# A perceiver block on one core: chunk 1's gathers behind the last gelu, chunk 0 sent to the scores first, two chunks' contexts loaded in four parts

## What is computed

```python
x = x + L0_xattn(layernorm(x), ctx, ctx, ...)        # 16 heads
x = x + L0_attn(layernorm(x), ...)                   # a state space convolution
# L0_ffn: the first mixture, 16 experts, each token goes to its best four
logits = -dist2(x, keys) + x @ rw.T + rb
topv, topi = jax.lax.top_k(logits, 4);  w = softmax(topv)
hidden = gelu(einsum('bld,efd->blef', x, w1) + b1)
exp_out = einsum('blef,edf->bled', hidden, w2) + b2
fused = sum(w[..., None] * take(exp_out, topi), axis=2);   x = x + fused
# L1_xattn: one head, masked, no projections
h = layernorm(x)
attn = softmax(where(mask == 0, NEG, h @ ctx.T / 16))
x = x + layernorm(attn @ ctx) * gamma + beta
x = x + L1_attn(layernorm(x), ...)                   # selective scan
x = x + L1_ffn(layernorm(x), ...)                    # 8 experts, best two, and a shared one
```

## Time and profile before

| | us |
|---|---|
| median of 3 runs (lowest, highest) | 712.33 (711.55, 713.86) |
| the profiled execution, its own time | 712.5 |
| its span, first to last instruction | 710.7 |
| outside the span | 1.8 |
| TensorE busy | 676.7 (95%) |
| VectorE, ScalarE, GpSimd busy | 543.6, 414.0, 452.4 |
| mean granted TensorE clock | 0.994 of full |

### The profile page before, as it was taken

One profiled execution on the slowest core, in us unless ns is written; L12 is line 12 of the kernel. 1 busy time (PEld: TensorE's weight loads), 2 busy tenths in 40 slices (PEclk: granted clock), 3 DMA queues, 4 the chain that ended last, 5 costly groups with the idle time before them and its releaser, 6 DMA issues.

```text
span 710.7 us, 15537 instructions
## 1 busy us (share of the span) xinstructions
PE 676.7 (95%) x5712; PEld 554.0 (78%) x5712; DVE 543.6 (76%) x1212; ACT 414.0 (58%) x790; POOL 452.4 (64%) x487
## 2 busy tenths in 40 slices
PE   6899999999999988999999999998899899999998
PEld 3677778777777767999999999996457456666787
DVE  5887878787889776577777777754647999998676
ACT  3665656656665653566667667641336886665441
POOL 4848635546487644888998787736315699898130
PEclk9999999999999998999999999999999999999999
DMA  8301101011006565899999989975874610001000
GB/s 343 129 2 61 61 1 59 6 53 60 0 0 252 209 242 240 317 365 414 422 348 331 347 334 333 346 305 193 325 310 156 249 51 1 0 1 46 1 0 30
DMA packets 20365, 123.38 MB, mean 174 GB/s; under 512 B 2304, under 2 KB 6672, under 8 KB 13008
## 3 DMA queue, kind: packets, MB, share of 16 engines
q1 hardware_dynamic: 17376, 114.59, 42.0%
q0 software_dynamic: 2928, 8.00, 3.1%
HBM read 111.77 MB, written 10.81 MB: 172 GB/s over the span
## 4 chain that ended last, share of the span: by engine, by line
PE 81%; DVE 9%; ACT 5%; issue 3%; POOL 1%; DMA 1%; DVEq 0%; SPq 0%; ACTq 0%; PEldq 0%; POOLq 0%
PE banks L2279 70%; PE banks L2347 8%; DVE shown L2145 2%; PE banks L2911 2%; ACT probs L1155 1%; DVE negmax_raw L1674 1%; PE banks L2588 1%; ACT banks L1445 1%; DVE banks L2152 1%; DMA table<-in_table 1%; DVE xn L1566 1%; PE banks L2747 0%; ACT turned_back L1456 0%; POOL q_heads_hi L713 0%; POOL rstd L701 0%
## 5 line engine op out<-in xcount | busy, mean ns | idle before, releaser
L2279 PE MATMUL banks<-xT,raw 128*128 128x128 f32 x992 | 150.5, 275 | 0.6 <-DVE xT L1932 0.6
L2279 PEld LDWEIGHTS banks<-xT,raw 128*128 128x128 f32 x992 | 133.6, 191 | 3.1 <-issue 1.3
L971 POOL TENSOR_TENSOR w_lo<-raw,w_hi 128x1024 fp32r<-128x1024 f32 x52 | 122.8, 2389 | 0.9 <-ACT w_hi L1275 0.5
L1306 ACT ACTIVATE banks<-banks,later 128x128 f32<-128x128 f32 x208 | 70.5, 340 | 58.1 <-PE banks L2279 56.3
L1938 DVE CAST mid_hi<-banks 128x128 fp32r<-128x128 f32 x208 | 60.2, 289 | 36.5 <-ACT banks L1306 34.4
L1185 ACT ACTIVATE probsT<-banks 128x512 f32<-128x512 f32 x68 | 40.1, 598 | 74.8 <-PE banks L2347 74.5
L1055 POOL TENSOR_TENSOR inject<-BCbc,drive 128x1024 f32<-128x1024 f32 x31 | 72.8, 2362 | 11.3 <-DVE shown L2145 6.5
L1155 ACT ACTIVATE probs<-banks,negmax 128x1024 f32<-128x1024 f32 x64 | 71.2, 1113 | 11.7 <-DVE negmax L1676 9.9
L1674 DVE TENSOR_REDUCE negmax_raw<-banks 128x1 f32<-128x1024 f32 x64 | 77.5, 1211 | 0.4 <-PE banks L2279 0.3
L2279 PE MATMUL banks<-w_hi,mid_hi 128*128 128x256 f32 x208 | 75.5, 363 | 0.0
L2347 PE MATMUL banks<-table,probs 128*128 128x128 f32 x512 | 69.6, 279 | 0.4 <-DVE probsT L1647 0.4
(11 more groups left out here) (362 smaller groups left out, 1707.7 us busy)
## 6 DMA issues: line engine op xcount, KB each, us to landing
raw<-in_w SPq DMA_DIRECT2D x31, 2048.0 KB, 10.0
ctx_raw<-in_ctxT SPq DMA_DIRECT2D x8, 1024.0 KB, 4.7
ctxT<-in_ctxT SPq DMA_DIRECT2D x4, 2048.0 KB, 8.8
ctxN<-in_ctxN SPq DMA_DIRECT2D x4, 2048.0 KB, 13.9
x_slots<-zero SPq DMA_DIRECT2D x1, 3968.0 KB, 12.5
y_slots<-y_tile POOLq DMA_DIRECT2D x29, 128.0 KB, 7.0
wf<-in_w SPq DMA_DIRECT2D x9, 384.0 KB, 5.9
BCbc<-bc_rows SPq DMA_DIRECT2D x6, 512.0 KB, 6.9
```

The costliest lines, as they stand in the source:

```text
L971: nc.gpsimd.tensor_tensor(w2_lo[i % WB][:, cols], raw[i % WB][:, EW // 2:][:, cols], w2_hi[i % 2][:, cols].bitcast(F32), ALU.subtract).the ...
L1306: nc.scalar.activation(to, held, ACT.Gelu, bias=b1[:, bass.ds(at + u, 1)]).then_inc(gelu_done, 1)
L2279: return nc.tensor.matmul(o, lhsT, rhs, start=start, stop=stop)
```

## The change

It edits four things, and the arithmetic is the same.

1. GpSimd: chunk 1's four gathers wait for all 248 gelus. The power of chunk 0 (`rstd_of(4, 0)`) moves from behind chunk 2's second gather to ahead of its first; the power of chunk 1 now stands behind chunk 2's second gather, and chunk 2's third and fourth gathers behind that power.
2. VectorE: `combine(1)` moves behind the end of chunk 0's norm (`arrive(0)`).
3. SyncE: T(1) is no longer issued at the stores but after `gathered[0]`.
4. SyncE: T(1), T(2) and N(1) are issued as four DMAs of 512 KB each. A part of T has runs of 2 KB (half the keys of one of two rows), a part of N runs of 4 KB, where one DMA had 8 KB for a partition and batch. The waits on them count 64 for the four in the place of 16.

The diff, cut to its core (the waits on T and N count `16 * CTX_T_PARTS[p]` and `16 * CTX_N_PARTS[p]` accordingly):

```diff
+CTX_T_PARTS, CTX_N_PARTS = (1, 4, 4, 1), (1, 4, 1, 1)
...
             def context_T(p):
-                sp.dma_start(ctxT2[p][:], d["ctxT"][2 * p:2 * p + 2].rearrange("b p c n -> p b c n"))\
-                    .then_inc(ctxT2_loaded[p], 16)
+                if CTX_T_PARTS[p] == 1:
+                    sp.dma_start(ctxT2[p][:], d["ctxT"][2 * p:2 * p + 2].rearrange("b p c n -> p b c n")).then_inc(ctxT2_loaded[p], 16)
+                    return
+                for b in range(2):
+                    for keys in (slice(0, KEYS // 2), slice(KEYS // 2, KEYS)):
+                        sp.dma_start(ctxT2[p][:, b, :, keys], d["ctxT"][2 * p + b][:, :, keys]).then_inc(ctxT2_loaded[p], 16)
...
+                for b in range(2):
+                    for of in (slice(0, KC // 2), slice(KC // 2, KC)):
+                        sp.dma_start(ctxN2[p][:, b, of, :], d["ctxN"][2 * p + b][:, of, :]).then_inc(ctxN2_loaded[p], 16)
...
                 if i == COLD - 1:
-                    sp.wait_ge(y_stored[i % YB], 16 * (i // YB + 1))
+                    sp.wait_ge(gathered[0], 16 * TOP0)
                     context_T(1)
...
             gather_rows(0)
+            pool.wait_ge(gelu_done, TILES * UNITS)
             gather_rows(1)
+            rstd_of(4, 0)
             pool.wait_ge(last_taken, last_before + LAST)
             gather_rows(2, range(2))
-            rstd_of(4, 0)
-            gather_rows(2, range(2, 3))
             rstd_of(4, 1)
-            gather_rows(2, range(3, TOP0))
+            gather_rows(2, range(2, TOP0))
             gather_rows(3)
...
             combine(0)
-            combine(1)
             add_sums(0, 1)
             norm_begin(4, 0)
             add_sums(1, TC)
+            arrive(0)
+            combine(1)
             norm_begin(4, 1)
-            arrive(0)
             arrive(1)
```

More of the change, by code:

```diff
@@ L599, in context_T @@
             def context_T(p):
-                sp.dma_start(ctxT2[p][:], d["ctxT"][2 * p:2 * p + 2].rearrange("b p c n -> p b c n"))\
-                    .then_inc(ctxT2_loaded[p], 16)
-            def context_N(p):
-                sp.dma_start(ctxN2[p][:], d["ctxN"][2 * p:2 * p + 2].rearrange("b p k n -> p b k n"))\
-                    .then_inc(ctxN2_loaded[p], 16)
+                if CTX_T_PARTS[p] == 1:
[4 more added lines that the diff above has]
+                        sp.dma_start(ctxT2[p][:, b, :, keys], d["ctxT"][2 * p + b][:, :, keys]).then_inc(ctxT2_loaded[p], 16)
+            def context_N(p):
+                if CTX_N_PARTS[p] == 1:
+                    sp.dma_start(ctxN2[p][:], d["ctxN"][2 * p:2 * p + 2].rearrange("b p k n -> p b k n")).then_inc(ctxN2_loaded[p], 16)
+                    return
+                for b in range(2):
+                    for of in (slice(0, KC // 2), slice(KC // 2, KC)):
+                        sp.dma_start(ctxN2[p][:, b, of, :], d["ctxN"][2 * p + b][:, of, :]).then_inc(ctxN2_loaded[p], 16)
             sp.wait_ge(pads_ready, 1)
@@ L2156, in _ @@
                     elif m == 0 and g <= SPLIT_ROWS:
-                        dve.wait_ge(c_landed[g - 1], raw_loads(1 + g) + 32)
+                        dve.wait_ge(c_landed[g - 1], raw_loads(1 + g) + 16 * CTX_T_PARTS[g] + 16)
                     elif m == 0:
@@ L2730, in score2 @@
                 k = p % 2
-                pe.wait_ge(ctxT2_loaded[p], raw_loads(p + 1) + 16)
+                pe.wait_ge(ctxT2_loaded[p], raw_loads(p + 1) + 16 * CTX_T_PARTS[p])
                 pe.wait_ge(early_ready, TC + p + 1)
@@ L2750, in mix2 @@
             def mix2(p):
-                pe.wait_ge(ctxN2_loaded[p], 48 if p == TC - 1 else 32)
+                pe.wait_ge(ctxN2_loaded[p], (32 if p == TC - 1 else 16) + 16 * CTX_N_PARTS[p])
                 pe.wait_ge(left2_ready, p + 1)
```

## The result

| | before | after |
|---|---|---|
| median, measured side by side, 16 runs each (lowest, highest) | 713.45 (711.55, 716.26) | 715.97 (713.51, 717.35) |
| ratio, 95% interval | | 1.0032 [1.0018, 1.0045] |
| the profiled execution, its own time | 712.5 | 715.07 |
| its span | 710.7 | 713.3 |
| mean granted TensorE clock | 0.994 | 0.995 |

The change makes the kernel slower by 0.32%, 2.3 us of the median and 2.6 between the two profiled executions. The interval reaches to both sides of 0.3%: that the kernel got slower is clear, whether by more than 0.3% is not. The two traces can be laid over each other without a shift: the first of ScalarE's two copies of the last tiles starts at 483.60 before and at 483.72 after.

What follows compares the result with a forecast made beforehand. TensorE was taken as the bound, held up by late signals to the gelus and by context loads. Loads 2.5 + 0.6 = 3.1 later, less slack 1.9, gave 1.2: 712.5 + 1.2 = 713.7, median 713.5, range 711.0 to 716.5.

Steps and rivals of the forecast that it cites:

- rival A: TensorE's signals late beside T(1) and chunk 1's gathers, 1.4 to 2.8 us slower: 714.9 to 716.3, chance 0.30.
- late loads set scores 3: T(3) lands 3.1 later against a slack of 1.9, so TensorE starts scores 3 1.2 later.
- one of its own signs of failure: The forecast fails if T(2) takes clearly more than 9.5 from first issue to last landing.
- The other signs: T(2) leaves at 502.5 to 503.5; TensorE idles about 2 ahead of mix 1, a little ahead of scores 3.
- the likeliest class: Whole kernel: time the same within 0.3%, chance 0.57, against faster 0.05 and slower 0.38.
- Late signals removed: From gelus to chunk 0's turn: gelus come in time, last sums at 490.7 not 492.37, 1.6 us gained.
- a pair, gathers and a load: End of the mixture: TensorE's signals reach ScalarE late, by some 4 us, while eight gathers and T(1) run together.
- Chunk 1's rows "are in" before VectorE wants them: On VectorE: the rows are in at 493.9, 2.9 after the last gather starts; combine(1) starts at 495.1.
- For T(1) the parts cost nothing: T(1) on SyncE: it starts at about 486 and is needed beyond 500, so its parts cost zero.
- Parts of T(2) and N(1): Context loads: four parts cost 0.5 for T(2) and 0.1 for N(1), 0.6 together, ends 0 to 1.6.
- My bound from the next stage's weights: Cost of parts: 2 MB take 5.78 at 363 GB/s, not 4.96 at 423, so 0.8 more per T.
- The queue behind chunk 1's power: On GpSimd: chunk 2's third and fourth gathers wait for chunk 1's power, so T(2) leaves 2.5 later.

Runs made afterwards that it cites:

- only_gelu_wait: The kernel before with one edit, chunk 1's gathers wait for the last gelu: 718.23, ratio 1.009 to the kernel before.
- only_t1_wait: The kernel before with one edit, T(1) waits for chunk 0's gathers: 716.42, ratio 1.0049 to the kernel before.
- t1_and_gelu_wait: The kernel before with both waits, T(1) behind chunk 0's gathers and chunk 1's gathers behind the last gelu: 717.52, ratio 1.0078.
- parts_off: The kernel after with T(1), T(2) and N(1) as one DMA each again: 714.65, ratio 1.0021 to the kernel before.
- only_parts: The kernel before with the four parts alone, waits and orders as before: 713.68, ratio 1.0019 to the kernel before.
- five_gathers: The kernel after with chunk 1's first gather issued directly behind chunk 0's four: 716.47, ratio 1.0036 to the kernel before.
- early_wait: The kernel after with chunk 1's gathers waiting for the fourth last gelu, not the last: 715.35, ratio 1.0025 to the kernel before.
- greatest_ahead: The kernel after with whole loads, chunk 2's four gathers ahead of chunk 1's power, and greatest(2) ahead of leave(0) on VectorE: 712.43, ratio 1.0002.
- greatest_again: The kernel of greatest_ahead run once more, unchanged: 711.35 beside 712.89 for the kernel before, ratio 0.9981.
- g2_ahead: The kernel after with all four gathers of chunk 2 ahead of chunk 1's power on GpSimd: 712.78, ratio 1.0003 to the kernel before.

## Why the prediction came out as it did

The forecast was 713.5 with its own range to 714.4, and the time 715.97 lies above that, inside the wide range of 711.0 to 716.5. That it lies inside is partly luck: the upper end was drawn for rival A, whose late signals did not come. The mechanism was the forecast's own (late loads set scores 3), but its terms were too small, and one of its own signs of failure came true: T(2) took 10.8 from its first issue, clearly more than 9.5. The other signs: T(2) left at 503.78, just outside 502.5 to 503.5; TensorE waited 1.45 ahead of mix 1 and 0.46 ahead of scores 3, each released by a load, where I had said about 2 and a little, and 1.64 ahead of scores 2, which I had not foreseen. Whether the likeliest class, no change within 0.3%, holds at 0.32% the interval leaves open.

- **Late signals removed: right.** Last sums 490.76 (forecast 490.7), turn at 495.63 (495.6), chunk 0's end on VectorE 495.05 (495.1).
- **Why they were late: half wrong.** I named a pair, gathers and a load. The load isn't needed: only_gelu_wait has the pair, with four gathers, and no late gelu; only_t1_wait has no load at the first late gelu and most of the delay (3.2 of 3.9 at the last gelu). The length of the row of gathers counts. Rival A with its 0.30 was built on the pair; its late signals between 489 and 495 did not come, beside T(1) and four gathers. Its price was misread too: the last gelu came 2.0, not 1.4, above the pitch behind the one ahead of it (2.49 of idle time against 0.51), and the 1.36 of the earlier trace rows is idle time, of which 0.85 is lateness.
- **Chunk 1's rows "are in" before VectorE wants them: wrong.** I took 2.9 from the last gather's start, a row of gathers that ran alone. Beside T(1) it was 495.90 - 491.35 = 4.5. That shifted the whole row by 0.8, and T(2) left 3.3 later instead of 2.5.
- **"For T(1) the parts cost nothing": wrong, and this is the same 0.8.** TensorE doesn't need T(1) early, but the gathers share the DMA engines with it. Among the kernels that have chunk 0 first, `combine(1)` waits 0.85, 2.21, 0.47 and 0.38 in the four with T(1) in parts and not at all in the five with it in one piece. Those rows were taken 10.1 to 11.4 after T(1)'s first issue; in only_t1_wait and t1_and_gelu_wait, where `combine(1)` waits beside a whole T(1), 9.2 after it. I had even written that short runs let a gather pass sooner; the rows came later beside them.
- **Parts of T(2) and N(1): 0.6 forecast, 1.1 measured** (20.8 against 19.7), 0.9 by parts_off and 1.6 by only_parts, where the slack covered it. My bound from the next stage's weights took runs of 3 KB for runs of 2 KB.
- **The queue behind chunk 1's power: right in kind.** Undone alone it gave back 2.1 us by the ratios, 1.3 by the trace at scores 3.
- **The wait ahead of mix 0 wasn't in the sum.** It grew from 0.83 to 1.73 in the profile, and to 2.20 to 2.84 in three sister kernels, with half clock behind it. The cause is late signals for the two copies `probsT` beside six gathers in a row: together they are 0.9, 1.4, 2.0 and 1.9 late in the kernel after, parts_off, five_gathers and early_wait, which is what the wait exceeds 0.83 by. Where the loads don't cover it, as in parts_off, it is what remains.
- **The sum with measured terms:** 3.3 + 1.1 - 1.9 = 2.5 in place of 1.2; 712.5 + 2.5 = 715.0, and the profiled execution took 715.07. The median of the 16 runs is 0.9 above it, where I had set 0.2 below. Five of those 16 have a mean granted clock of 0.988 or 0.989 and times from 716.0 to 717.4, and five more are at 0.990; of the 34 runs of the kernel before beside the last four experiments nine are at 0.990 and none is below. The profile of greatest_ahead is at 0.990 with half clock only far ahead of the passage (264 to 278); those of five_gathers and early_wait, at 0.988, have that and half clock in mix 0. So half clock in mix 0 would fit the runs below 0.990; no trace of the kernel after shows it, and so this is argued only.

In the Trainium skill, "DMA: Bandwidth & Descriptors", section "Bandwidth", advises at least 1 MiB for a DMA. Its figures stand there for DMAs that GpSimd issues, and these loads are SyncE's. By my estimate from that page T would have taken 12.8; T(2) left at 503.78, and scores 2, which waited for it, began at 514.60, 10.8 later, where a whole T takes 8.8. The measurement lies in the middle: the rule had the right sign, and the estimate, with a fixed cost for one part after another, was 2.0 too long.

## What to carry to other kernels

A load that its own reader doesn't need soon still has a price if something urgent shares the DMA engines with it; cost it by the one who waits for the urgent transfer. When an edit puts a wait into a shared queue, follow the chain from there through every engine's order, and ask at each step what stands directly behind; here the gain of 1.6 was real, and a power that stood between two gathers was enough to take back about as much (1.3 by the trace, 2.1 by the ratios). And when one lateness is mended, look for the next in order before looking at the clock: the load, then a maximum behind a norm, were each hidden by the one before.

## What the runs showed of the hardware

**Long rows of gathers delay TensorE's signals.** In the kernel before, in only_parts and in only_t1_wait, with eight indirect DMAs in a row (one each 1.26), ScalarE's gelus were late from the fifth on: issued at 484.30 in only_t1_wait, where the last gelu on time starts at 484.88. The delays came to 3.9 for the last gelu before (490.78 against 486.85 by the pitch). Six in a row, between 499.6 and 509 in the kernel after, parts_off, five_gathers and early_wait, went with the copies of `probsT` 0.9 to 2.0 late in sum; in greatest_again, where a power lies between each four, they are 0.2 late. Rows of four gathers delayed no gelu, and one later signal by 0.5 in early_wait, where the pause between two fours was 1.2. The number isn't a rule for every indirect DMA: beside the scatters at the mixture's start the gelu at 295.04 was 0.84 late in a row of four. Nor do the runs tell the count of gathers from the time that a row lasts, since all of them are 1.26 apart. A load beside the row isn't needed. Which resource is shared, no run shows.

**Rows gathered beside a load come in about when the load does.** Alone the last gather of a chunk took 2.9. Beside T(1) it took 4.5 in the kernel after, 5.8 in g2_ahead, 7.0 in only_t1_wait and 7.1 in early_wait, but from T(1)'s first issue the rows took 9.1 to 9.6 where T(1) was whole (8.8 for the load itself: before, only_gelu_wait, only_t1_wait, t1_and_gelu_wait) and 10.1 to 11.4 where it was in parts (the kernel after, g2_ahead, five_gathers, early_wait, only_parts). An earlier gather, as in early_wait, didn't bring them in earlier.

**Half clock after short waits.** In this passage TensorE fell to 1.2 GHz (granted clock 0.50) at or behind waits of 2.20, 2.70, 2.84, 3.28, 4.05 and 4.49, and not behind 1.73; each fall cost 1.4 to 1.9 in the product behind it.
